# A GRU step on one core: the reset gate taken from its tanh inside a three-element scan

## The reference, cut to what matters

```python
def cell(h, x):
    gi = x @ W_ih + b_ih
    gh = h @ W_hh + b_hh
    i_r, i_z, i_n = jnp.split(gi, 3, axis=-1)
    h_r, h_z, h_n = jnp.split(gh, 3, axis=-1)
    r = jax.nn.sigmoid(i_r + h_r)
    z = jax.nn.sigmoid(i_z + h_z)
    n = jnp.tanh(i_n + r * h_n)
    h_new = (1.0 - z) * n + z * h
    return (h_new, h_new)

x = x + attention(x, cond_2048, ...)
_, hs = jax.lax.scan(cell, cond_2048, x over time)
x = x + hs
```

## Time and profile before

| What | Value |
|---|---|
| median of three runs | 2333.5 us |
| profiled execution: its time, its span | 2333.61 us, 2331.5 us |
| attention and set-up, until the matmuls that open the GRU's banks | 0 to 628.30 us |
| first matmul of the step loop | 651.30 us |
| busy share PE, DVE, ACT, POOL | 95%, 64%, 55%, 9% |
| granted TensorE clock, over the run | 0.993 |
| `wih`: from issue to landing | 14.6 us |

### The profile page before, as it was taken

How to read it: one execution, slowest core, us unless ns; L and a number is a source line. 1 busy time by engine, 2 the same in 40 slices (tenths; PEclk the granted TensorE clock), 3 DMA queues, 4 the chain that set the end, 5 groups by cost and what they waited for, 6 DMA issues and landing times.

```text
span 2331.5 us, 131690 instructions
## 1 busy us (share of the span) xinstructions
PE 2211.1 (95%) x58512; PEld 1738.9 (75%) x58512; DVE 1499.1 (64%) x5745; ACT 1291.0 (55%) x5178; POOL 203.0 (9%) x223
## 2 busy tenths in 40 slices
PE   5999999999799999999999999999999999999988
PEld 3766657666477888878788887878788788888776
DVE  3776867768456666666666666666666666666665
ACT  3766747657245555555555555555555555555554
POOL 4314233233200000000000000000000000000000
PEclk9999999999999999999999999999999999999999
DMA  6000000000110000000000000000100000000000
GB/s 208 2 1 19 2 19 1 1 1 1 65 34 22 17 27 16 24 21 23 28 16 26 18 27 17 27 19 21 28 16 26 18 26 18 26 19 21 25 5 13
DMA packets 41097, 55.12 MB, mean 24 GB/s; under 512 B 9424, under 2 KB 34000, under 8 KB 40528
## 3 DMA queue, kind: packets, MB, share of 16 engines
q1 hardware_dynamic: 34112, 38.81, 5.3%
q0 software_dynamic: 1584, 7.73, 0.9%
q10 hardware_dynamic: 4832, 0.15, 0.1%
HBM read 29.90 MB, written 16.78 MB: 20 GB/s over the span
## 4 chain that ended last, share of the span: by engine, by line
PE 81%; DVE 7%; ACT 7%; issue 2%; ACTq 1%; DMA 1%; POOLq 1%; POOL 0%; SPq 0%; DVEq 0%
PE ps L476 53%; PE ps L462 7%; PE ps L356 6%; PE ps L307 6%; DVE rT L840 2%; PE ps L400 2%; PE ps L383 2%; PE ps L342 2%; PE ps L449 2%; DVE xb L835 2%; ACT r_pair L645 2%; ACT r_pair L642 2%; ACT xb L653 2%; DVE v_pair L825 2%; ACT probs L610 1%
## 5 line engine op out<-in xcount | busy, mean ns | idle before, releaser
L476 PE MATMUL ps<-wqkv,xb 128*4 128x128 f32 x49152 | 1489.5, 273 | 52.2 <-DVE xb L835 39.7
L476 PEld LDWEIGHTS ps<-wqkv,xb 128*4 128x4 f32 x49152 | 1216.4, 87 | 336.7 <-DVE xb L835 310.5
L840 DVE STREAM_TRANSPOSE rT<-ps 128x128 f32<-128x128 f32 x512 | 162.0, 316 | 342.3 <-PE ps L476 342.2
L642 ACT ACTIVATE r_pair<-rT 128x16 f32<-128x16 f32 x512 | 112.3, 219 | 456.1 <-DVE rT L840 456.1
L651 ACT ACTIVATE t_z<-znT 128x8 f32<-128x8 f32 x1024 | 214.6, 210 | 251.3 <-DVE znT L820 251.3
L820 DVE STREAM_TRANSPOSE znT<-ps 128x128 f32<-128x128 f32 x1024 | 312.2, 305 | 63.2 <-PE ps L476 0.9
L835 DVE TENSOR_TENSOR_SCAN xb<-z_trip,xb 128x24 f32<-128x24 f32 x1024 | 212.9, 208 | 120.5 <-ACT xb L653 2.9
L653 ACT ACTIVATE xb<-v_pair 128x16 f32<-128x16 f32 x1024 | 222.9, 218 | 52.3 <-DVE v_pair L825 1.3
L825 DVE TENSOR_TENSOR_SCAN v_pair<-r_pair,znT 128x16 f32<-128x16 f32 x1024 | 196.0, 191 | 71.1 <-ACT r_pair L645 1.4
L462 PE MATMUL ps<-wih,x1T 128*32 128x256 f32 (+1 forms) x4096 | 231.9, 326 | 0.1
L831 DVE TENSOR_SCALAR z_trip<-t_z 128x8 f32<-128x8 f32 x1024 | 177.8, 174 | 26.1 <-ACT t_z L651 0.6
(11 more groups left out here) (82 smaller groups left out, 1323.1 us busy)
## 6 DMA issues: line engine op xcount, KB each, us to landing
gi_spill<-gi_image SPq DMA_DIRECT2D x64, 192.0 KB, 2.1
seeds<-gi_spill SPq DMA_DIRECT2D x228, 32.0 KB
seeds<-gi_spill SPq DMA_DIRECT2D x284, 16.0 KB
xb<-in_x SPq DMA_DIRECT2D x4, 1024.0 KB, 5.8
out<-xb SPq DMA_DIRECT2D x64, 64.0 KB, 2.2
wqkv<-in_L_cond_W_qkv SPq DMA_DIRECT2D x1, 3072.0 KB, 12.7
wih<-in_L_cond_W_ih POOLq DMA_DIRECT2D x1, 3072.0 KB, 14.6
wqkv<-in_L_cond_W_hh POOLq DMA_DIRECT2D x1, 3072.0 KB, 10.6
```

Source lines behind the costliest of these rows:

```text
L476: last = nc.tensor.matmul(ps[QD * j:QD * j + B, bank, 0:P], hist_flat[:, first:first + 3 * B - 2:3], weights, start=False, stop=False, ski ...
L840: nc.vector.transpose(rT[:], ps[:, r_bank, 0:P]).then_inc(s["rT_ready"], 1)
```

## The change

The reset gate's affine instruction (L645) is gone. With t = tanh(x/2), r = (1 + t)/2, so 2 (i_n + r h_n) = 2 i_n + h_n + t h_n. The scan now runs over three elements a value: data0 is (0, 1, h_n), data1 is (1, t, 2 i_n), so its states are 1, 1 + t and (1 + t) h_n + 2 i_n. The tanh behind it takes half of that (`scale=0.5`). So 2 i_n is needed: the candidate's columns of `wih` are doubled on GpSimd, in four pieces of 128x512 during batch 1 of the attention, and the candidate's part of the bias `b_in` on VectorE.

The constants of the two operands lie in a new tile `zn_terms`, [half, row group, a, entry, 3]; the transposes of z and n write only its every third element, and tanh of r writes into the middle ones. `znT`, `r_pair` and `v_pair` are gone, `v_trip` holds the scan's result. The candidate waits on `tr_done` (tanh of r) in place of `r_ready_gru`, and the two waits in front of it have changed places.

```diff
         rT = sb("rT", [P, P])
-        znT = sb("znT", [P, 2, P])
-        r_pair = sb("r_pair", [P, 16, 2])
-        v_pair = sb("v_pair", [P, 16, 2])
+        zn_terms = sb("zn_terms", [P, 2, 4, 2, 16, 3])
+        v_trip = sb("v_trip", [P, 16, 3])
...
+                    if b == 1 and n % 4 == 1:
+                        if n == 1:
+                            await_on_pool(ld_wih, 16)
+                        nc.gpsimd.tensor_scalar(wih[:, n // 4, 2 * D:3 * D], wih[:, n // 4, 2 * D:3 * D], 2.0, None,
+                                                ALU.mult).then_inc(s["wih_doubled"], 1)
...
-            pe.wait_ge(ld_wih, 16)
+            pe.wait_ge(s["wih_doubled"], KT)
...
                 act.wait_ge(s["rT_ready"], step + 1)
-                nc.scalar.activation(r_pair[:, :, 1].rearrange("p (c b) -> p c b", b=B), rT[:].rearrange("p (c r) -> p c r", r=QD)[:, :, 0:B],
+                nc.scalar.activation(zn_terms[:, :, 0, 1, 8:16, 1].rearrange("p h (k b) -> p h k b", b=B),
+                                     rT[:].rearrange("p (h k r) -> p h k r", h=2, r=QD)[:, :, :, 0:B],
                                      ACT.Tanh, scale=0.5).then_inc(s["tr_done"], 1)
-                act.wait_ge(s["tr_done"], step + 1)
-                nc.scalar.activation(r_pair[:, :, 1], r_pair[:, :, 1], ACT.Copy, bias=0.5,
-                                     scale=0.5).then_inc(s["r_ready_gru"], 1)
...
-                    nc.scalar.activation(t_z[:, half, :], znT[:, half, 0:16:2], ACT.Tanh, scale=0.5).then_inc(s[tz_name], 1)
+                    nc.scalar.activation(t_z[:, half, :], zn_terms[:, half, 0, 0, 0:8, 2], ACT.Tanh, scale=0.5).then_inc(s[tz_name], 1)
...
-                                         v_pair[:, 8 * half:8 * half + 8, 1].unsqueeze(2).broadcast_to([P, 8, 2]),
-                                         ACT.Tanh).then_inc(s[n_name], 1)
+                                         v_trip[:, 8 * half:8 * half + 8, 2].unsqueeze(2).broadcast_to([P, 8, 2]),
+                                         ACT.Tanh, scale=0.5).then_inc(s[n_name], 1)
...
-            nc.vector.memset(r_pair[:], 0.0)
+            nc.vector.tensor_scalar(b_in[:, 2 * P:3 * P], b_in[:, 2 * P:3 * P], 2.0, None, ALU.mult).then_inc(s["bias_ready"], 1)
+            nc.vector.memset(zn_terms[:].rearrange("p h r a e s -> p (h r a e s)"), 1.0).then_inc(s["terms_set"], 1)
+            dve.wait_ge(s["terms_set"], 1)
+            for half in range(2):
+                nc.vector.memset(zn_terms[:, half, 0, 0, :, 0], 0.0)
...
                 def transpose_zn(half, bank):
                     return nc.vector.transpose(
-                        znT[:, half, :].rearrange("p (r k b s) -> p k r s b", r=4, k=4, b=B, s=2), ps[:, bank, 0:P])
+                        zn_terms[:, half, :, :, :, 2].rearrange("p r a (k b) -> p k r a b", b=B), ps[:, bank, 0:P])
 
                 def candidate(half):
-                    first = 16 * half
                     return nc.vector.tensor_tensor_scan(
-                        v_pair[:].rearrange("p e s -> p (e s)")[:, first:first + 16],
-                        r_pair[:].rearrange("p e s -> p (e s)")[:, first:first + 16],
-                        znT[:, half, 16:32], 0.0, ALU.mult, ALU.add)
+                        v_trip[:, 8 * half:8 * half + 8, :].rearrange("p e s -> p (e s)"),
+                        zn_terms[:, half, 0, 0, 8:16, :].rearrange("p e s -> p (e s)"),
+                        zn_terms[:, half, 0, 1, 8:16, :].rearrange("p e s -> p (e s)"), 0.0, ALU.mult, ALU.add)
...
-                dve.wait_ge(s["r_ready_gru"], step + 1)
                 dve.wait_ge(s["znaT_ready"], step + 1)
+                dve.wait_ge(s["tr_done"], step + 1)
                 candidate(0).then_inc(s["va_done"], 1)
```

More of the change, by code:

```diff
@@ L159, in attention_gru_kernel @@
             "rexp_done", "rtr_done", "r_ready", "pv_done", "oT_ready", "ox_ready", "y_done", "x1_ready",
-            "bias_ready", "seeds_clear", "hid_n_ready", "pairs_ready", "banks_open", "gi_done", "gi_evac", "seeded", "h_a", "h_b",
-            "r_sum", "zna_sum", "znb_sum", "rT_ready", "znaT_ready", "znbT_ready", "tr_done", "r_ready_gru", "va_done", "vb_done",
+            "bias_ready", "terms_set", "seeds_clear", "hid_n_ready", "pairs_ready", "banks_open", "gi_done", "gi_evac", "seeded", "h_a", "h_b",
+            "r_sum", "zna_sum", "znb_sum", "rT_ready", "znaT_ready", "znbT_ready", "tr_done", "va_done", "vb_done", "wih_doubled",
             "tza_done", "tzb_done", "za_done", "zb_done", "na_done", "nb_done", "out_added", "rows_ps", "rows_ready")}
@@ L809, in add_out @@
                 last.then_inc(s["out_added"], 1)
-            dve.wait_ge(s["bias_ready"], 1)
+            dve.wait_ge(s["bias_ready"], 2)
             for n, b in ((0, 0), (0, 1), (0, 2), (0, 3), (1, 0)):
```

## The result

The changed kernel takes 2355.15 us (median of four runs, 2354.71 to 2357.53), the kernel before 2333.95 us beside it: ratio 1.0095, 95% interval 1.0083 to 1.0108. It is slower by 21 us, where 12.6 us less were forecast. The span of its profiled execution is 2353.4 us, at a granted clock of 0.994.

The account below looks back on a forecast made before the run. The prediction took a ring of dependent small instructions, not TensorE, to bound each step. 2333.6 us - 12.8 (512 steps x 0.025 us) + 0.2 (doubling on GpSimd) = 2321.0 us, 0.5% faster; range 2313 to 2331 us.

Parts of the forecast that it names:

- What bounds the kernel: In each step, a ring of waiting VectorE, ScalarE and TensorE instructions sets the time, 3.26 us; TensorE has 0.40 us slack.
- The z branch decides, 0.025 us a step: Half a: the unshortened tanh and gate of z end last, so the new state gains only 0.025 us, 12.8 us in all.
- The whole affine: Rival: the affine's full time on the chain is gained, 0.25 us a step, 128 us, giving 2206 us; chance 0.01.
- the candidate's 0.07 us: Half a: without the affine the candidate starts 0.04 us after the transpose's end, about 1011.35 in place of 1011.42.
- The scan of 24 elements: The candidate's scan, 24 elements in place of 16, takes 0.21 us in place of 0.19, 0.02 us more.
- half b's cover: Half b: the scan's extra 0.02 us is hidden under the z branch, by 0.03 us, so it costs nothing.
- The transposes and the reads at a stride of 12 bytes: Both z and n transposes of a step, writing every third element, and the z tanh's reads were priced at 0.
- the sign: The prediction is wrong if half a's new state starts under 0.86 or over 0.89 us after its transpose.
- the row of L808: Output addition reading far-apart elements: 0.74 ns an element extra, 95 ns for a transpose of 128; set aside as a longer-stride read.
- two memsets: Nearest rows for writes at the new stride: 16 elements 72 ns, 32 adjacent 85 ns, leaving nothing for the stride.
- The rival: Transposes pay for the lines they cross: 95 ns more each, 165 ns a step net, 84 us, giving 2418 us; chance 0.06.
- Doubling on GpSimd: Four weight-doubling operations in batch 1, 0.9 us each (bounds 0.62 and 1.55); the first delays a norm, costing 0.2 us once.

Follow-up runs that it names:

- three kernels (2321, 2320, 2281 us): Changed kernel with z and n transposed into a compact tile again, 2321.37 us; kernel before with reset gate by sigmoid, 2320.24 us, with both gates by sigmoid, 2281.13 us.
- Two different kernels with both: Changed kernel with z and n transposed into a compact tile again, 2321.37 us; kernel before with the reset gate by one sigmoid and the waits swapped, 2320.24 us.
- the compact transposes: Changed kernel with z and n transposed into a compact tile as before; the scan reads constants, so only its time counts: 2321.37 us, ratio 0.9943 to the kernel before.
- the isolated transposes: Kernel before with isolated 128x128 transposes in several write patterns behind its last step; durations only: about 316 ns, 345 to 353 ns, 399 to 412 ns.
- the alternating patterns: Kernel before with isolated transposes behind its last step that fill 32 adjacent 16-byte lines but change line with every value: 407 to 410 ns, adjacent 315 ns.

## Why the prediction was wrong, point by point

- *What bounds the kernel*: right. A ring of small instructions with slack on TensorE; a shorter ring went through to the time in three kernels (2321, 2320, 2281 us).
- *The z branch decides, 0.025 us a step*: right, as a price of the affine's removal and the swapped waits together. Two different kernels with both gained 13.6 us (the ratio 0.9943 with the compact transposes, the medians 2334.97 and 2321.37) and 13.8 us (2333.99 and 2320.24), where 12.8 were worked out. The whole affine, 128 us, was never there. But the prediction booked the candidate's 0.07 us under the affine alone. It took the transpose's way to the candidate as 0.04 us, as in half b, where one wait stands, and had no term for the swap that makes it so in half a. The run with the old order shows that this term is large: 22.5 us.
- *The scan of 24 elements, half b's cover*: right, 208 ns and hidden.
- *The transposes and the reads at a stride of 12 bytes*: this step failed. It was taken at 0 and measures 337 - 305 = 32 ns for each of 1024 transposes, 33 us, and 213 against 210 ns for the z tanh behind each [page of the changed kernel against that of before], some 3 us. 33 + 3 - 13 = 23 us, measured 21. The prediction had named the sign: half a's new state over 0.89 us after its transpose. It is at 0.91 us on average.
- *Why it was mis-sized*: the row of L808 had the right price, 0.74 ns an element; the isolated transposes with a crossing at each value give (408 - 315)/128 = 0.73 ns. I let two memsets of the kernel before overrule it, since they write at exactly this stride. Of the four operations that were written at several strides they are the only one that doesn't show it (165 ns at strides 1 and 4), and copies, which do, had no row at that stride. The equal times of the r transpose and the z and n transpose proved less than I took from them: the fragments of before put two values in a row into the same 16 bytes, and so stood on the free side of the edge.
- *The rival*: right in mechanism, at 0.06 with far too small a chance, and too dear in size, 84 us, because I let every value pay in full. At 12 bytes one value in four shares 16 bytes with the one before, and the estimate behind the alternating patterns makes 38 ns of that in place of 95; the transposes of the kernel paid 32. The rule from the Trainium skill that I had beside it (SBUF — State Buffer, section "Door 1: The DMA port swizzle"), at least two hits to 16 bytes, said on which side of the edge the new pattern lies; the levels of 316, 345 to 353 and 408 ns agree with it for copies and transposes. The alternating patterns (407 and 410 ns) agree as well: the hits have to come in a row, and the same note does speak of consecutive accesses.
- *Doubling on GpSimd*: 1.52 us an operation, the upper bound, not 0.9. The norm came late and VectorE waited. At most 0.2 us of it reached the loop: before the doubling GpSimd's work on the norms already ran 0.51 us earlier than in the kernel before (185.35 against 185.86 us), and the loop starts 0.31 us earlier. The first r transpose starts at 653.22 us in the changed kernel:

```profile
653.22 0.32 DVE L845 STREAM_TRANSPOSE rT<-ps 128x128 f32<-128x128 f32 x1 [8.75 <-PE ps L480]
```

In the kernel before it starts at 653.53:

```profile
653.53 0.32 DVE L840 STREAM_TRANSPOSE rT<-ps 128x128 f32<-128x128 f32 x1 [8.59 <-PE ps L476]
```

## What to carry to other kernels

Before pricing the removal of a link of a chain, find the branch that runs beside it and read how far behind it is: here 0.23 us of work, together with the swap of two waits, was worth 0.025 us. And where two waits stand in front of the next link, look which of them comes last before giving a gain to the work removed. When a change moves a value's place in memory, price every instruction that writes it, most of all one on the critical ring, and count how many values in a row fall into the same 16 bytes. Between a row of another operation at the same stride and a row of a worse stride, keep both as live cases.

## What the runs showed of the hardware

- VectorE's fp32 writes to SBUF: free where two values in a row share 16 bytes (315 to 318 ns for a transpose). Where none do, a transpose takes 0.73 ns more a value, a copy 0.71 ((382 - 291)/128), a product 0.41 ((280 - 227)/128), a memset nothing. At 12 bytes a transpose takes 0.23 to 0.30 ns more ((345 - 315)/128, (353 - 315)/128). A tile that is filled completely still costs the full price if the order of the writes alternates between 16-byte lines (407 and 410 ns). Reads from SBUF at a stride of 16 bytes cost a product 0.34 ns a value ((272 - 228)/128), reads of PSUM at strides of up to 16 bytes cost a copy nothing (291 ns).
- Of two waits in front of an instruction the one attached to it is cheaper when it comes last: the candidate started 0.03 us after the transpose's end with it attached, 0.10 us with it as an instruction of its own. In a loop of 512 dependent steps the order of two lines was 22 us (2355.15 against 2377.65).
